# Routed FFN on one core: the logits' bias copied into PSUM by ScalarE ahead of the products, and the second logits product split over two halves of TensorE's rows

## The reference, cut to what matters

```python
lr = xf @ m1                                         # 256 -> 64
mask_logits = jnp.einsum('bl,lxy->bxy', lr, m2) + mb # 64 -> 16 groups of 64, plus bias
quant_mask = jnp.argmax(mask_logits, axis=-1)        # one unit of each group
mid = jnp.einsum('ai,aji->aj', xf, w1p[j, quant_mask])
res = jnp.einsum('ai,aij->aj', relu(mid), w2p[j, quant_mask]) + b2
x = x + 0.5 * res                                    # xf is the layernorm of x
```

## Time and profile before

| | us |
|---|---|
| median of 3 runs (range) | 3364.06 (3362.36 to 3365.32) |
| the profiled execution | 3363.8 |
| its span | 3362.1 |
| PE busy | 3140.9 (93%) |
| DVE busy | 2654.7 (79%) |
| ACT busy | 1644.0 (49%) |

### The profile page before, as it was taken

The page is one execution under the profiler, slowest core; times in us unless marked ns, Lnnn a source line. Parts: engine busy times, 40 slices in busy tenths (PEclk is TensorE's granted clock), DMA queues, the critical chain, the costliest instruction groups (busy, mean ns, idle before and its releaser), DMA issues. The chain is left out here.

```text
span 3362.1 us, 102510 instructions
## 1 busy us (share of the span) xinstructions
PE 3140.9 (93%) x36736; PEld 2710.0 (81%) x36736; DVE 2654.7 (79%) x4369; ACT 1644.0 (49%) x4554; POOL 1313.5 (39%) x2170
## 2 busy tenths in 40 slices
PE   5999999999979999789999999999799999999999
PEld 4888888898865665578887877887688888988888
DVE  7999999999943323278877878877699999999998
ACT  3333333333336556577777777777433333333332
POOL 3333333333323433255555555555433333333332
PEclk9999999999989999899999999999899999999999
DMA  3111111111125555433333333333211111111111
GB/s 85 58 56 52 56 56 56 52 56 56 52 92 196 200 197 195 169 99 103 97 100 103 103 102 97 100 103 103 69 52 56 56 56 51 56 56 54 53 56 46
DMA packets 224965, 290.57 MB, mean 86 GB/s; under 512 B 25460, under 2 KB 191732, under 8 KB 224888
## 3 DMA queue, kind: packets, MB, share of 16 engines
q1 hardware_dynamic: 224888, 289.52, 27.2%
HBM read 171.97 MB, written 117.44 MB: 86 GB/s over the span
## 5 line engine op out<-in xcount | busy, mean ns | idle before, releaser
L578 PE MATMUL mid_ps<-xT_hl,w_hl 128*128 128x128 f16 x12288 | 730.4, 219 | 0.0
L425 PE MATMUL res_ps<-w_hl,midT_hl 128*128 128x256 f16 x6144 | 712.5, 273 | 1.2 <-DVE x_out L546 1.2
L578 PEld LDWEIGHTS mid_ps<-xT_hl,w_hl 128*128 128x128 f16 x12288 | 699.7, 98 | 0.5
L382 POOL TENSOR_TENSOR var_eps<-moments,eps_col 128x1 f32<-128x1 f32 x384 | 110.4, 287 | 1420.0 <-DVE moments L378 1420.0
L425 PEld LDWEIGHTS res_ps<-w_hl,midT_hl 128*128 128x128 f16 x6144 | 590.4, 98 | 65.5 <-DVE midT_hl L533 1.7
L486 ACT ACTIVATE midT_hl<-mid_ps 128x1024 f16<-128x1024 f32 x256 | 261.9, 1023 | 686.4 <-PE mid_ps L589 686.4
L512 DVE TENSOR_TENSOR_SCAN runmax<-restart,logits_ps 128x1024 f32<-128x1024 f32 x256 | 585.5, 2287 | 8.3 <-PE logits_ps L567 0.4
L397 ACT ACTIVATE xn_hl<-xc,rstd 128x256 f16<-128x256 f32 x384 | 194.0, 505 | 475.0 <-POOL rstd L387 386.9
L372 DVE BATCH_NORM_STATS2 stats<-x_in 128x6 f32<-128x256 f32 x384 | 162.0, 422 | 294.0 <-DMA x_in<-x 289.3
L517 DVE TENSOR_TENSOR step<-runmax 128x1024 bf16<-128x1024 f32 x256 | 315.0, 1230 | 8.9
L533 DVE SCALAR_TENSOR_TENSOR midT_hl<-mid_ps,midT_hl 128x1024 f16<-128x1024 f32 x256 | 311.9, 1218 | 7.5 <-ACT midT_hl L486 7.5
(11 more groups left out here) (143 smaller groups left out, 6253.6 us busy)
## 6 DMA issues: line engine op xcount, KB each, us to landing
projected<-qkfv_out SPq DMA_DIRECT2D x128, 512.0 KB, 2.9
qkv<-projected SPq DMA_DIRECT2D x128, 384.0 KB, 3.4
x<-x_out SPq DMA_DIRECT2D x256, 128.0 KB, 1.7
x_in<-x SPq DMA_DIRECT2D x256, 128.0 KB, 2.2
x_res<-x SPq DMA_DIRECT2D x256, 128.0 KB, 2.1
x_in<-in_L_attn_x SPq DMA_DIRECT2D x128, 128.0 KB, 2.1
x_res<-in_L_attn_x SPq DMA_DIRECT2D x128, 128.0 KB, 2.1
gate<-projected SPq DMA_DIRECT2D x128, 128.0 KB, 3.1
```

Source lines behind the costliest of these rows:

```text
L425: last = nc.tensor.matmul(dst, left(lp, k), right(rp, k), start=(k == 0 and lp == rp), stop=(k == blocks - 1 and lp == 1))
L578: nc.tensor.matmul(mid_ps[t.slot][:, cols], w1_hl[:, wp, k, cols], xT_hl[:, t.ring, xp, k], start=(c % PER_BANK == 0 and k == 0 and wp == xp),
```

## The change

The bias leaves the second product. `mb` is loaded as 128 equal rows (`mb_rows`), scaled once by VectorE, and a new ScalarE stage `seed_logits` copies it into both banks of `logits_ps` for tile s+2 at the end of each step, as soon as the scan of the tile before is done. All logits products then add to what lies there. To set the banks' accumulate state, TensorE makes two matmuls at the start of each phase, and ScalarE waits for them.

The second product keeps its 64 rows of m2's low part alone. Its left operand is doubled (`low_h2`: `low_hl`'s high part on all 128 rows, made before `low_low` turns the lower half of `low_hl` into the low part), m2's low part as well (`m2_low2`), and the two column halves are multiplied on different halves of the rows: bank 0 on rows 0 to 63, bank 1 on rows 64 to 127. The two first products now come one after the other, then the two second ones. In TensorE's list `low_rank` comes ahead of `mask_logits`. `low_low` waits for both ScalarE copies.

```diff
-        m2_low_mb = sb("m2_low_mb", [P, d_ff], f16)
+        m2_low2 = sb("m2_low2", [P, d_ff], f16)
+        mb_rows = sb("mb_rows", [P, d_ff])
...
-                    sp.dma_start(mb_f[:, :], a["mb"].rearrange("(a x) y -> a (x y)", a=1)).then_inc(loaded["mb"], 16)
+                    sp.dma_start(mb_rows[:, :], a["mb"].rearrange("(a x) y -> a (x y)", a=1).broadcast_to([P, d_ff])
+                                 ).then_inc(loaded["mb"], 16)
...
-                    sp.wait_ge(mb_chain, 5)
-                    sp.wait_ge(consts_set, 1)
-                    sp.dma_start(m2_low_mb[d_low:d_low + 3, :], mb_parts[0:1, :, :]).then_inc(mb_rows_placed, 16)
-                    sp.wait_ge(mb_rows_placed, 16)
...
-                    nc.vector.tensor_scalar(mb_parts[:, 0], mb_f[:, :], S_LOW, None, ALU.mult).then_inc(mb_chain, 1)
...
-                    nc.vector.tensor_copy(mb_parts[:, 2], mb_rest[:, 1]).then_inc(mb_chain, 1)
+                    nc.vector.tensor_scalar(mb_rows[:, :], mb_rows[:, :], S_LOW * S_LOW, None, ALU.mult)
...
                 def _(act):
+                    act.wait_ge(logits_opened, 1 if base == 0 else 2)
...
+                    def seed_logits(t):
+
+                        after(act, runmax_made, t, lag=1)
+                        nc.scalar.activation(logits_ps[:, :], mb_rows[:, :], ACT.Copy).then_inc(logits_seeded, 1)
...
-                        nc.scalar.activation(low_h1[0:d_low, t.slot], low_ps[0:d_low, :],
-                                             ACT.Copy).then_inc(low_h1_made, 1)
+                        nc.scalar.activation(low_h2[:, t.slot], low_ps, ACT.Copy).then_inc(low_h2_made, 1)
...
-                                   (evacuate_xT, 3)],
+                                   (evacuate_xT, 3), (seed_logits, 2)],
...
                     def low_low(t):
                         after(dve, low_high_made, t)
+                        after(dve, low_h2_made, t)
...
+                    for c in range(2):
+                        last = nc.tensor.matmul(logits_ps[:, c * BANK:(c + 1) * BANK], m2_high2[:, 0:P],
+                                                m2_high2[:, 0:BANK], start=True, stop=True)
+                    last.then_inc(logits_opened, 1)
+
                     def mask_logits(t):
 
                         after(pe, low_low_made, t)
-                        after(pe, low_h1_made, t)
-                        after(pe, runmax_made, t, lag=1)
+                        after(pe, low_h2_made, t)
+                        after(pe, logits_seeded, t)
                         for c in range(2):
                             cols = slice(c * BANK, (c + 1) * BANK)
                             nc.tensor.matmul(logits_ps[:, cols], low_hl[:, t.slot], m2_high2[:, cols],
-                                             start=True, stop=False)
-                            last = nc.tensor.matmul(logits_ps[:, cols], low_h1[:, t.slot], m2_low_mb[:, cols],
-                                                    start=False, stop=True)
+                                             start=False, stop=False, skip_group_check=True)
+                        for c in range(2):
+                            cols = slice(c * BANK, (c + 1) * BANK)
+                            rows = slice(c * d_low, (c + 1) * d_low)
+                            last = nc.tensor.matmul(logits_ps[:, cols], low_h2[rows, t.slot], m2_low2[rows, cols],
+                                                    start=False, stop=True, skip_group_check=True)
                         last.then_inc(logits_done, 1)
...
-                    pipeline(pe, [(mask_logits, 1), (low_rank, 2), (up, 0), (pick, 0), (transpose_x, 3),
+                    pipeline(pe, [(low_rank, 2), (mask_logits, 1), (up, 0), (pick, 0), (transpose_x, 3),
                                   (down, -1)],
```

More of the change, by code:

```diff
@@ L172, in build @@
         step = sb("step", [P, GROUPS, d2 + 2], bf16)
-        low_h1 = sb("low_h1", [P, 2, P], f16)
+        low_h2 = sb("low_h2", [P, 2, P], f16)
         names = ["w1", "w2", "m1", "m2", "mb"]
         loaded = {n: sem(f"loaded_{n}") for n in names + ["b2", "wqkfv", "wo", "g"]}
-        mb_rows_placed = sem("mb_rows_placed")
         ident_zeroed, ident_made = sem("ident_zeroed"), sem("ident_made")
         far_zeroed = sem("far_zeroed")
-        consts_set = sem("consts_set")
         highs_made, lows_made = sem("highs_made"), sem("lows_made")
-        mb_chain = sem("mb_chain")
         masks_zeroed, masks_made, wo_scaled = sem("masks_zeroed"), sem("masks_made"), sem("wo_scaled")
@@ L193, in build @@
             m2_f = st("m2_f", [P, d_ff])
-            mb_f = st("mb_f", [1, d_ff])
-            mb_rest = st("mb_rest", [1, 2, d_ff])
-            mb_parts = st("mb_parts", [1, 3, d_ff], f16)
             b2_f = st("b2_f", [P, d_model])
@@ L310, in _ @@
                     nc.vector.memset(step[:, :, :], 0.0)
-                    nc.vector.memset(m2_low_mb[d_low:P, :], 0.0).then_inc(consts_set, 1)
-                    nc.vector.memset(low_h1[d_low:P, :, :], S_LOW)
                     dve.wait_ge(loaded["mb"], 16)
-                    nc.vector.tensor_scalar(mb_parts[:, 0], mb_f[:, :], S_LOW, None, ALU.mult).then_inc(mb_chain, 1)
[L316 to L323, removed]
-                    nc.vector.tensor_copy(mb_parts[:, 2], mb_rest[:, 1]).then_inc(mb_chain, 1)
+                    nc.vector.tensor_scalar(mb_rows[:, :], mb_rows[:, :], S_LOW * S_LOW, None, ALU.mult)
                     dve.wait_ge(highs_made, 1)
@@ L329, in _ @@
                     dve.wait_ge(highs_made, 2)
-                    nc.vector.scalar_tensor_tensor(m2_low_mb[0:d_low, :], m2_f[0:d_low, :], S_LOW,
-                                                   m2_high2[0:d_low, :], ALU.mult, ALU.subtract)
+                    nc.vector.scalar_tensor_tensor(m2_low2[:, :], m2_f[:, :], S_LOW, m2_high2[:, :],
+                                                   ALU.mult, ALU.subtract)
                     dve.wait_ge(highs_made, 3)
@@ L596, in low_rank @@
                         after(pe, low_low_made, t, lag=1)
-                        after(pe, low_h1_made, t, lag=1)
+                        after(pe, low_h2_made, t, lag=1)
                         three(low_ps, lambda p, k: m1_hl[:, p, k], lambda p, k: xT_hl[:, t.ring, p, k],
@@ L1241, in build @@
         low_done, low_high_made = sem("low_done"), sem("low_high_made")
-        low_h1_made, low_low_made = sem("low_h1_made"), sem("low_low_made")
+        low_h2_made, low_low_made = sem("low_h2_made"), sem("low_low_made")
+        logits_opened, logits_seeded = sem("logits_opened"), sem("logits_seeded")
         logits_done, runmax_made, step_made = sem("logits_done"), sem("runmax_made"), sem("step_made")
```

## The result

| | before | changed |
|---|---|---|
| median of 20 runs (range), us | 3365.45 (3362.36 to 3374.24) | 3375.41 (3371.8 to 3380.01) |
| the profiled execution, us | 3363.8 | 3377.23 |
| its span, us | 3362.1 | 3375.0 |

The ratio is 1.003, with a 95% interval of 1.0023 to 1.0037: the changed kernel is 10 us slower. That is inside the predicted range (3360 to 3391) and 7 us above the predicted time. And it is inside the range only because I had stretched the range for a rival, the exposed weight load, that did not happen: the forecast's own range ended at 3374.

The account below looks back on a forecast made before the run. TensorE's own instructions were taken to bound the FFN phases. From 3363.8 us, +1.5 (logits' matmuls), +1.9 (setup) and +0.7 (phase start) gave 3367.9, say 3368 us; range 3360 to 3391, some 0.85.

Parts of the forecast that it names:

- the exposed weight load: Rival, 64-row pair: weight load exposed as with fp32, 0.10 instead of 0.01 us a step, +23 us, 3391; chance 0.10.
- the forecast's own range: Whole kernel: 3360 to 3374 us, from the ends of the forecast's terms, without the rivals.
- The logits' four matmuls: FFN step on TensorE: pair's gain paid back by two changes of rows, 0.869 against 0.863 us, +1.5 us for 256 steps.
- ScalarE's copy in the steady step: FFN step on ScalarE: the copy takes 1.02 us, ends 0.4 us before TensorE wants it, and costs nothing.
- The moved stages: FFN step: low_rank 0.86 us earlier, low_low some 0.2 us sooner, logits complete 0.33 us later; no VectorE wait added.
- Setup: Before the first phase: 512 KB mb transfer ahead of the last weights, 1.5 to 2.7 us, taken as 1.9.
- Phase start: First steps of both FFN phases: first scan about 38.75 instead of 38.40, +0.7 us in all, between nothing and 2.
- A reading of little weight: First FFN phase's window: TensorE busy 940 of 960 us, granted clock 0.99, VectorE 851, ScalarE 332.
- the free change of rows: Rival, logits' matmuls: changing rows costs little, the step saves 0.2 us, 3319; chance 0.05.
- the late copy: Rival, FFN steps: ScalarE's copy is late for TensorE; at 0.2 us beyond its slack, 3419; chance 0.06.

Follow-up runs that it names:

- interleaved: Changed kernel with the mb transfer last and each bank's second product right behind its first, four changes of rows a step; 3486.29 us, ratio 1.0351.
- mb_by_pe: Changed kernel with mb loaded as one 4 KB row that TensorE spreads in setup, and low_high ahead of the norm's high part; 3369.24 us, ratio 1.0008.
- split_alone: Changed kernel with the mb transfer last, no bias, ScalarE copy or opening matmuls, and mask_logits ahead of low_rank; 3369.11 us, ratio 1.0011.

## Why the prediction was half right

- **The logits' four matmuls: right, and shown.** Predicted 0.869 us, measured 0.849 up to the first `up` matmul and 0.01 of exposed weight load behind it; the distances came out as predicted, 0.31, within 0.02, and 0.32, and so did the pair's first duration, 0.39 us. The 9 ns between the sums are the stagger (4 ns instead of 9) and 4 ns on the way back (0.319 and 0.010 instead of 0.322 and 0.011). The predicted +1.5 us is -0.8. That the changes of rows and the pair cancel is shown from three sides: without the split the step is 7.168, with four changes 7.587, with half the changes 7.058.
- **ScalarE's copy in the steady step: right.** 1.04 us for 1.02, early by 0.54 for 0.4, nothing waits.
- **The moved stages: right in the steady step.** No wait of VectorE was added.
- **Setup: mis-sized, +6.1 us for +1.9.** The step of the prediction that failed is "512 KB at 340 to 197 GB/s". With the load added to the kernel before, it is 5.4 us by the profile and 6.0 by the medians, above the range's 2.7. I had taken the added transfer to move at the rate of its neighbours. With it the lowest rate was 143 GB/s instead of 197, but a low of 140 shows without it as well, and setups without it end up to 2.9 us apart (26.5 to 29.4): my rates came from one profile, and the earlier trace rows show two windows of it, not the spread.
- **Phase start: mis-sized.** The two FFN phases together are 4.2 us longer; with the 0.8 that the steps give back, 5.0 us lie at their starts and ends, where I had 0.7. The first scan is 0.5 us late in each, near the predicted 0.35, but I stopped at the first scan. Two more steps of the start wait for ScalarE's copy, and `low_rank` waits for its input ahead of `mask_logits`; the price stood in TensorE's waits.
- **Projection and attention: +1.5 us, not foreseen.** Most of it (1.0 us) is in the projection, and it goes with ScalarE's copy or its opening matmuls: from the projection's first statistics to the end of its last matmul it takes 436.0 to 436.4 us in the four profiles of kernels without them, 437.1 to 437.9 in the ten with them. The cause is open.
- **A reading of little weight.** The window of the earlier trace rows runs some 56 us into the projection; the step that I went by is well inside the first phase.

None of the rivals happened. The exposed weight load is excluded by the pair's 387 ns, the free change of rows by `interleaved`, the late copy by the 4.3 us in total. The forecast's own upper end, 3374, would have needed all my terms at their ends; the measured one is 1.4 us above it (0.9 above the unrounded 3374.5). What stays open is why the transfer costs three times its bytes at the rates before, why setup ends at 29.4 us without it in `mb_by_pe`, and the 1.0 us of the projection.

## What to carry to other kernels

Two 64-row matmuls on different row halves run together, but the way there and back costs about 0.1 us each: a single pair of 512 columns breaks even, and only a second pair between the same two changes earns anything. A price that a foreign phase of the same trace shows, down to the distance of two starts, held to 10 ns in the new place; the terms that I had taken from averages (a rate, a first scan) were the ones that missed. In a kernel of steady steps, cost the setup and the first steps by TensorE's waits there: a copy that costs nothing in the steady step was waited for three times at the start. And before a difference of some us in an untouched phase is left unexplained, look at the granted clock there, stretch by stretch.

## What the runs showed of the hardware

A weight load of 64 rows in fp16 takes 93 ns, as short as one of 128 rows (98), so the change of rows exposes only some 10 ns of it. Changing rows costs the same behind 512 columns (0.311 - 0.216 = 0.095 us) as behind 128. The Trainium skill, "TensorEngine Tiling (Array Packing)", Key Properties, has this as a drain at each change of mode, and "TensorE: Matmul & The Clock Gate", Part 3, has the 4 ns between tiles of a pack; the 4 ns of the pair agree. Not expected was the load of 128 equal rows: 512 KB cost 5.4 us of setup, where their bytes at 197 GB/s are 2.7. And the attention, untouched, together with the projection, took 1462 to 1465 us in twelve profiles and 1469 and 1473 in two. These two have a stretch early in the attention at the lower of TensorE's two clock levels (granted clock 0.50, 1.2 instead of 2.4 GHz). From 1424 to 1441 us, right before it in `split_alone`, TensorE was busy for 14.6 us at the higher level; the kernel before, busy for 14.8 us there, kept that level.
